# Self-attention heads stacked by transfers instead of by selection matmuls, with a new lead-in order

## The reference, cut to what matters

```python
q = (h @ wq + bq).reshape(B, N, 16, 16)      # k and v likewise
scores = einsum("bqhd,bkhd->bhqk", q, k) / 4 # 1024 x 1024 for each head
out = einsum("bhqk,bkhd->bqhd", softmax(scores), v).reshape(B, N, 256) @ wo + bo
```

## Time and profile before

| | |
|---|---|
| Median of 3 runs | 3698.08 us (3683.58 to 3699.18) |
| Time of the profiled execution | 3701.89 us |
| Its span | 3700.1 us |
| Mean granted TensorE clock | 0.963 of full |
| Busy: PE, DVE, ACT, POOL | 92%, 60%, 62%, 24% |

### The profile page before, as it was taken

The page is one execution under the profiler, slowest core; times in us unless marked ns, Lnnn a source line. Parts: engine busy times, 40 slices in busy tenths (PEclk is TensorE's granted clock), DMA queues, the critical chain, the costliest instruction groups (busy, mean ns, idle before and its releaser), DMA issues.

```text
span 3700.1 us, 60840 instructions
## 1 busy us (share of the span) xinstructions
PE 3394.4 (92%) x22433; PEld 2000.9 (54%) x22433; DVE 2223.0 (60%) x3645; ACT 2302.2 (62%) x3983; POOL 871.0 (24%) x578
## 2 busy tenths in 40 slices
PE   8999998999899898998998889989998899899988
PEld 6767766444643564446444744455446444564465
DVE  2323324794397556953794559746955488549654
ACT  2333332787578555875786457865875578658764
POOL 0322322103400431015103420052024200340061
PEclk8989989999999999999999999999999999999999
DMA  5011012110100001110010010100100101000100
GB/s 184 1 36 35 2 36 63 32 16 26 39 8 14 13 13 57 14 30 31 13 16 15 12 57 11 22 26 26 14 19 13 58 7 26 24 28 11 22 13 13
DMA packets 226988, 101.25 MB, mean 27 GB/s; under 512 B 159951, under 2 KB 210322, under 8 KB 226582
## 3 DMA queue, kind: packets, MB, share of 16 engines
q1 hardware_dynamic: 201734, 77.21, 8.4%
q10 hardware_dynamic: 24976, 20.15, 1.8%
HBM read 79.31 MB, written 9.96 MB: 24 GB/s over the span
## 4 chain that ended last, share of the span: by engine, by line
PE 79%; DVE 12%; ACT 5%; issue 2%; POOL 1%; DMA 0%; SPq 0%; ACTq 0%; DVEq 0%; POOLq 0%
PE ps L736 76%; DVE mxh L1791 4%; PE ps L1184 2%; DVE ctxk L1740 2%; DVE ow L1823 1%; ACT probs L1470 1%; DVE tok L1526 1%; PE ps L1045 1%; DVE small L1510 1%; DVE x L1757 1%; DVE mx L1788 1%; POOL small L1847 1%; ACT qs L1439 1%; ACT whole L1424 1%; ACT hT L1256 1%
## 5 line engine op out<-in xcount | busy, mean ns | idle before, releaser
L1470 ACT ACTIVATE probs<-ps 128x512 f32<-128x512 f32 (+1 forms) x2176 | 1220.4, 639 | 222.3 <-PE ps L736 169.7
L1791 DVE TENSOR_REDUCE mxh<-ps 128x2 f32<-128x1024 f32 x1024 | 1232.1, 1220 | 101.2 <-PE ps L736 96.3
L736 PE MATMUL ps<-probs,v 128*32 128x256 f32 (+2 forms) x8064 | 732.8, 435 | 9.7 <-ACT probs L1470 6.3
L736 PE MATMUL ps<-ks,qs 64*128 64x512 f32 x2048 | 502.4, 491 | 51.5 <-DVE mxh L1791 23.3
L736 PEld LDWEIGHTS ps<-ks,qs 64*128 64x128 f32 x2048 | 193.0, 183 | 445.8 <-issue 347.7
L736 PE MATMUL ps<-qs,ks 64*128 64x512 f32 x2048 | 425.5, 413 | 4.0 <-DVE mxh L1791 3.0
L1911 POOL TENSOR_TENSOR hT<-hT,tok 128x512 f32<-128x512 f32 (+1 forms) x32 | 40.9, 1279 | 1221.1 <-DMA tok<-weights_of_outputs 1221.1
L736 PEld LDWEIGHTS ps<-probs,v 128*32 128x32 f32 (+1 forms) x8064 | 160.0, 107 | 302.7 <-ACT probs L1470 249.1
L736 PEld LDWEIGHTS ps<-qs,ks 64*128 64x128 f32 x2048 | 244.0, 184 | 127.6 <-ACT probs L1470 105.9
L1788 DVE TENSOR_REDUCE mx<-ps 128x4 f32<-128x312 f32 x384 | 166.3, 477 | 150.9 <-PE ps L736 147.4
L736 PE MATMUL ps<-hT,slot 128*128 128x512 f32 x448 | 235.5, 659 | 21.2 <-issue 8.5
(11 more groups left out here) (226 smaller groups left out, 5893.9 us busy)
## 6 DMA issues: line engine op xcount, KB each, us to landing
qs<-mx SPq DMA_DIRECT2D x896, 0.5 KB, 2.0
slot<-in_L_w SPq DMA_DIRECT2D x8, 1024.0 KB, 10.0
slot<-in_L_fc_w SPq DMA_DIRECT2D x8, 1024.0 KB, 5.2
hT<-ow SPq DMA_DIRECT2D x48, 128.0 KB, 2.7
tok<-weights_of_outputs SPq DMA_DIRECT2D x192, 32.0 KB, 1.9
xin<-in_x ACTq DMA_DIRECT2D x5, 1024.0 KB, 5.9
x_after_block<-x ACTq DMA_DIRECT2D x20, 256.0 KB, 2.3
xin<-x_after_block SPq DMA_DIRECT2D x5, 1024.0 KB, 5.5
```

What stands on the lines that cost most here:

```text
L736: return pe.matmul(out, lhsT, rhs, start=start, stop=stop)
L1470: ins = act.activation(dst, src, ACT.Exp, scale=SCALE)
L1791: dve.tensor_reduce(mxh[:, z, t, j // 2, j % 2, :], ps[:, a:a + 2, :], AX.X, ALU.max, negate=True).then_inc(dve_done, M.add(dve_done, name))
```

## The change

In each self-attention:

- Only the stacks of heads 0 to 3 (pairs 0 and 1) are still made by matmuls: 8 of 32. The other 24 are filled by transfers from SP (send_heads, step X), straight from the rounded and difference tiles: part 1 for heads 4 to 7 (after the 9th A), part 2 for heads 8 to 15 (four steps, each after one "both" of (1, 0)). So that the source rows lie in the right order, the columns of the weights and biases are permuted on the host (heads_apart).
- A stack has 48 rows of data, the maximum's row is 48 (32 before); the row of ones in ks comes from a constant tile (ones).
- The rounded and difference tiles have places of their own: those of heads 0 to 7 in probs buffers 2 and 3, those of heads 8 to 15 in slots 2 and 3. So the exponentials of unit 2 wait for part 1, and the MLP's weights are loaded by SP after it has waited for the landing of part 2.
- The first A needs only the stacks of pair 0; the 16 A of (0, 0) take key half 0 first, then key half 1. P for heads 0 to 7, second half, stands after the 2nd and 4th A, its K after the 6th and 8th, V 0 after the 9th.
- The four P of heads 8 to 15 stand in units 3 to 6 (the 4th to the 7th).
- Before the first S, A may use all eight banks.

Elsewhere: in cross-attention OT stands at the end of the unit; ahead of an MLP two up steps stand before T 1, ScalarE writes the exact copy of a channel block right after its rounded one, and the second reciprocal root comes after the splitting of the first half.

```diff
-            ("K", "dddd", "q", 0, 0), ("K", "aaaa", "k", 0, 0), ("P", "k", 0, 1), ("P", "q", 0, 1), ("V", 0), ("K", "ddaa", "k", 0, 1), *[("mask",)] * first)
+            ("K", "dd--", "q", 0, 0), ("K", "aa--", "k", 0, 0), *[("mask",)] * first)
...
+        moves = [("X", 2, which, e) for e in range(2) for which in "qk"]
...
+                if (g, n) == (0, 0):
+                    maxima += [("A", g, n, t, j) for i in range(2) for t in range(TPH) for j in (i, 2 + i)]
...
+                    if (g, n) == (1, 0):
+                        last += moves[t:t + 1]
...
+        beside = {2: [("P", "k", 0, 1)], 4: [("P", "q", 0, 1)], 6: [pair_of("k", 1)], 8: [pair_of("q", 1)],
+                  9: [("X", 1, which, e) for e in range(2) for which in "qk"] + [("V", 0)], 17: [("add",)]}
+        in_unit = dict(enumerate([("V", 1), ("V", 2), ("V", 3), ("P", "q", 1, 0), ("P", "k", 1, 0), ("P", "q", 1, 1), ("P", "k", 1, 1)]))
...
+                def send_heads(tag, part, which, e):
+
+                    moved, c = group_moved if part == 1 else heads_moved, part - 1
+                    end = (tag, part) if (which, e) == ("k", 1) else None
+                    for n in range(NH):
+                        sp.wait_ge(pool_done, upto(pool_done, (tag, "P", which, c, n)))
+                    if which == "k":
+                        pairs = slice(PAIRS // KC // 2, PAIRS // KC) if part == 1 else slice(PAIRS // KC, PAIRS)
+                        sp.dma_start(ks[stacked(e, MAXROW, MAXROW + 1), pairs, :].bitcast(F32), ones[0:(pairs.stop - pairs.start) * N // 32, :]
+                                     ).then_inc(moved, M.add(moved, None, LOADED))
+                    for i, (dst, src) in enumerate(heads_of(tag, which, part, e)):
+                        sp.dma_start(dst, src).then_inc(moved, M.add(moved, end if i == 2 else None, LOADED))
+                    if part == 2 and end:
+                        sp.wait_ge(heads_moved, upto(heads_moved, end))
+                        for dst, s, name in (W1, 2, {"L1sa": "L1_w1", "L2sa": "L2_fc1_w"}[tag]), (W2, 3, {"L1sa": "L1_w2", "L2sa": "L2_fc2_w"}[tag]):
+                            then = tag[:2] + "mlp"
+                            sp.dma_start(dst, wide(T[name])).then_inc(slot_loaded[s], M.add(slot_loaded[s], then, LOADED))
...
-            if u > lag:
-                put(tag, ("OT",) + units[u - lag - 1][:2])
             if u >= lag:
                 put(tag, ("PV",) + units[u - lag], ("O",) + units[u - lag][:2])
             if u < len(units):
                 put(tag, ("S",) + units[u] + (2,), *last[4 * u + 2:4 * u + 4])
+            if u > lag:
+                put(tag, ("OT",) + units[u - lag - 1][:2])
...
+                            if g == 1:
+                                pe.wait_ge(group_moved, upto(group_moved, (tag, 1)))
+                            elif g > 1:
+                                pe.wait_ge(heads_moved, upto(heads_moved, (tag, 2)))
...
+                        if not cross and (u, j) == (PROBS_KEPT, 0):
+                            act.wait_ge(group_moved, upto(group_moved, (tag, 1)))
```

More of the change, by code:

```diff
@@ L166, in more @@
                 taken += 1
-        first_slot = GH * TPH
-        for i in range(first_slot):
-            more(i + 1)
-            put(tag, *[w for w in beside[i:i + 1] if w])
-        more(first_slot + 1)
-        put(tag, *beside[first_slot:], ("add",))
-        lead = first_slot + 4
-        more(lead)
+        lead = GH * TPH + 4
+        for i in range(1, lead + 1):
+            more(i)
+            put(tag, *beside.get(i, []))
         lag = 2
@@ L271, in cross_attention @@
         put(tag, ("o", 2), ("o", 3))
-        put(follow, ("T", 0), ("N", 1), ("T", 1), *[("up", 0, m) for m in range(FM)])
+        put(follow, ("T", 0), ("N", 1), ("up", 0, 0), ("up", 0, 1), ("T", 1), *[("up", 0, m) for m in range(2, FM)])
     def mlp(tag, follow):
@@ L334, in constant_rows, with heads_apart @@
     return out
+def heads_apart(a, blocks):
+    import numpy as np
+    columns = np.arange(a.shape[-1])
+    for block in range(blocks):
+        for first, heads in ((P // 2, GH), (P, 2 * GH)):
+            at = block * D + first
+            columns[at:at + heads * HD] = at + np.arange(heads * HD).reshape(heads, HD).T.ravel()
+    return a[..., columns]
 def selections():
@@ L343, in selections @@
         out[2 * HD * pp, NSEL, [MASKROW, STACK + MASKROW]] = 1.0
-    for which, places in (("q", ((0, 16), (48,))), ("k", ((0, 48), (16,)))):
+    for which, places in PLACES.items():
         for part in range(2):
@@ L407, in build @@
         assert at[0] <= r2_end
+        kept = {(which, 0): [place(f"{which}0{part}", [P, N], F32R, offset=r2 + 4 * (PROBS_KEPT * GH * HALF + (2 * i + k) * N))
+                             for k, part in enumerate("hl")] for i, which in enumerate("qk")}
         at[0] = r2
@@ L446, in build @@
         hTl0 = place("hTl0", [P, KC, N], F32R, offset=at[0])
+        kept.update({(which, 1): [place(f"{which}1{part}", [P, N], F32R, offset=at[0] + 4 * (2 * 2048 + (2 * i + k) * N))
+                                  for k, part in enumerate("hl")] for i, which in enumerate("qk")})
         slot = [place(f"slot{i}", [P, 2048]) for i in range(4)]
@@ L1032, in _ @@
                         pe.wait_ge(SLOT_OF[tag], upto(SLOT_OF[tag], LAST_LOAD[tag]))
-                    if kind in ("begin", "load", "mask", "N", "add", "O", "R", "W", "Q", "both", "zero", "context", "out", "split"):
+                    if kind in ("begin", "load", "mask", "N", "add", "O", "R", "W", "Q", "both", "zero", "context", "out", "split", "X"):
                         continue
```

100 lines of the change are left out of this document (59 added, 41 removed).

## The result

The changed kernel takes 3877.35 us (median of 4, 3858.55 to 3881.19), the kernel before 3690.83 beside it (4 runs, 3678.11 to 3699.18): ratio 1.0491, 95% interval 1.0465 to 1.0517. It is 4.9% slower. The forecast was 3678, the range ended at 3722. The profiled execution took 3876.58 us with a span of 3874.8.

What follows compares the result with a forecast made beforehand. Self-attention's units were taken as full on TensorE and VectorE, its lead as paced nearly by VectorE. Self-attention +4, cross-attention -20 and MLP -4 us summed to -20: 3678 us against the median 3698.08; range 3638 to 3722.

Steps and rivals of the forecast that it cites:

- rival 3: Self-attention: part 2 delays small sums and maxima, reciprocals wait 2 and 7 us; slower, 3726 us; chance 0.18.
- First reduction: Self-attention's lead-in: the first reduce comes 8.4 us earlier, as removed selection matmuls stood before it.
- The lead: Self-attention, first reduce to M: VectorE paces 16 A at 1.2 us; 20.2 us, so 3.1 less.
- Projections in the units: Self-attention, units 3 to 6: four P at 1.92 us go where both engines are full; +7.5 us.
- The clock in units 0 to 2: Self-attention: half clock expected at the first S costs units 0 to 2 +1.5 us (0 to 3).
- SyncE's queue and the stops: Self-attention after the projections: sums of (0, 1) go out late, VectorE's reciprocal waits 1.6 to 4.9 us, taken as 3.
- They land 3.6 us later: SP's queue sum: the sums of (0, 1) go out at 34.0 us and land at 37.6 (35.7 to 39.0).
- The price of a stop: Self-attention's full units: added TensorE work or a stop of VectorE costs its full length; 3 us taken.
- Cross-attention: OT at the unit's end removes two thirds of TensorE's 31.7 us of waits for ow: -20 us (0 to -31.7).
- MLP: Before the MLPs: up steps start some 2 us earlier, gaining 0 to 1 us each; -4 us over eight.
- signs of being right: Earlier first reduce, longer units 3 to 6, 1.6 to 4.9 us DMA idle, half clock at first S, no ow wait.
- sign of being wrong: Self-attention: among others, the lead stays above 22 us because P and K chains hold up A.

Runs made afterwards that it cites:

- part 2 small: Changed kernel with part 2 moving 64 of 1024 columns, heads 8 to 15 reading the stacks of heads 0 to 7; 3785.39 us, ratio 1.026.
- every third row: Changed kernel with a stack's three 16-row shares laid row by row in turn, so transfers write spread rows; 3820.91 us, ratio 1.0332.

## Why the prediction was wrong

The time lies 155 us above the range. (The range itself ended at 3722, below the 3726 of its own rival 3.) By the prediction's own terms, in us an attention:

- **First reduction**, forecast -8.4: measured -8.3. Right in size, but not a gain by itself. With the selections kept (47.7 against 47.9 us to the first S) it is worth nothing, since TensorE's work up to the first S sets the end.
- **The lead**, -3.1: measured +0.5. I had VectorE pace it at 1.2 us an A; with 12.7 of 23.8 us at half clock TensorE holds it up. With the removed selection matmuls back the grant was 0.94, with only the projections back 6.8 to 10.2 us stayed at half clock. I looked for half clock only at the end of it.
- **Projections in the units**, +7.5: measured 7.6, and 10.6 us again when they were taken out.
- **The clock in units 0 to 2**, +1.5: measured +3.6.
- **SyncE's queue and the stops, +3.0: this is the step that failed.** Units 7 to the last A are 23.1 us longer. The stop is at (0, 0) and not at (0, 1). The rate of a large transfer, between 290 and 126 KB/us, was read from transfers to 64 and more partitions; to 16 it is about 105 KB/us with all DMA engines taken, and queued as they are they need 7.2 to 9.3 us from issue to landing, where the forecast's own bounds give 2.0 to 3.1. "They land 3.6 us later" took 1.7 us for the landing of one of them from a quiet machine; in the middle of part 2 it was 10.4. The reciprocal of (0, 0), put at "nothing", waited 8.7 to 9.2 us in all eight attentions, that of (0, 1), put at 3, in two. The sum over SyncE's queue counted who issues when, and not who lands when. (It is also loose in itself: 1.1 us and 0.9 to 2.0 are 2.0 to 3.1 together, not 1.4 to 3, and 37.6 less 34.1 is 3.5, where I took 3; neither matters here.) The queue step itself was sound: with part 2's bytes gone, the second reciprocal waits 3.5 us on average.
- **The price of a stop.** I priced it at its length. Units 7 to 15 lost 13.1 us for a stop of 8.5, because half clock follows, and more is lost behind them. In the six attentions with that one stop alone, the whole loss was 16 to 35 us. With part 2 small, stops of up to 5.4 us came with 7.5 us more in units 16 to 23 and 7.3 behind them.
- **Cross-attention**, -20: 21 measured alone. **MLP**, -4: about 10, from overlapping intervals.

SBUF - State Buffer, "Door 1: The DMA port swizzle", of the Trainium skill gave 104 GB/s for such a transfer, and the trace agrees (96 to 110). I had quoted it and made 1 us more of stop out of it. Its rate was right; I looked only at the landing of part 2 and not at what waits behind it. The same rule has rows spread over the stack reach more ports, which fits the direction of the run with every third row; it gave 124 GB/s, far from double.

Rival 3 named the mechanism, and its trigger, a stop over 5.5 us, was met. Its price of 3726 is 151 us short. It had 9 us of waits in an attention, 2 at (0, 0) and 7 at (0, 1); measured were 79.2/8 = 9.9, nearly all at (0, 0). So the waits were nearly right in sum, and what is missing is the half clock behind them, in the lead-in and in units 0 to 2.

Of the signs of being right, the first reduce, units 3 to 6 and the clock at the first S came as named. The idle with a DMA as releaser was 9 us at (0, 0), and 2.43 and 4.97 at (0, 1), where 1.6 to 4.9 was named; before OT 6.6 us of waiting were left. One sign of being wrong came too: the lead stayed above 22 us, at 23.8. P and K were named as the reason, and half of it was at half clock.

Open: why half clock lasts 24 us behind one stop and 68 behind another of the same length; why units 0 to 2 are 3 us longer with the lead-in's order, the add early and no transfers; and which of the twelve transfers' properties (16 partitions, 4 KB rows, both) sets 105 GB/s.

## What to carry over

A transfer that takes all DMA engines is a cost to every small transfer in flight, and here it was so from either queue: add up engine time (bytes by the rate for that shape) over the stretch, and look for the smallest transfer that a full engine waits for. At each of three places in the queue, something else paid for the 30 us: the sums, the maxima, or A itself. A stop of TensorE can't be priced at its length: 8.5 us cost 16 to 35. A transfer that a busy engine issues costs that engine the issue, 0.6 us each for ScalarE here. Matmuls taken from a stretch that is paced by another engine are no gain if the grant falls with them; and earlier first work is only worth what it takes off the engine that sets the end.

## What the runs showed of the hardware

- Half clock outlasts its cause with TensorE full: 62.50 of 62.50 us busy at 0.50 behind a stop of 8.6 us in the fourth attention. Behind six stops of 8.1 to 8.6 us it lasted 24, 68, 24, 44, 68 and 27 us, counted from where it begins in the stop.
- While SyncE's queue moved 256 KB transfers, a 2 KB one from ScalarE's queue needed 8.0 to 9.1 us, one from SyncE's own 10.4 (the sums of (0, 0), first attention); 1.7 us in the kernel before.
- Four small transfers issued by ScalarE took 2.5 us of it.
- VectorE's 128x16 maximum took 4.32 us in place of 0.19 beside GpSimd's add of 128x2048. SBUF - State Buffer, "SBUF: two separate sides", of the Trainium skill says that a VectorE instruction with two inputs in SBUF and a GpSimd one that reads SBUF exclude each other for the whole instruction; the trace agrees, in all eight attentions.
